# Layer-0 attention on one core: in each step of TensorE's loop the weighted sums are issued after the first score matmul, where they stood after the second

## The chip, the cores and the metric

The kernel runs on one core of one Trainium2 chip. The metric is the device time of one launch in microseconds. Lower is better. The kernel before has a median of 871.83 us over 3 runs.

## What is computed

The program is a two-layer block on an input of 2 x 1024 x 256. Layer 0 is a layer norm, an attention with 16 query heads of width 16 that share 8 key/value heads, and beside it a gated feed-forward whose weights are looked up in a table of 16 values. Layer 1 is a recurrence and a mixture of experts. Only the attention of layer 0 is touched:

```python
q = compute_rope(q); k = compute_rope(k)            # B, S, 16, heads
scores = einsum('bsdkg,btdk->bkgst', q, k) / sqrt(256)
w = softmax(scores, axis=-1)
ctx = einsum('bkgst,btdk->bkgsd', w, v)
```

and what reads it: the output projection, `x = x + s * silu(ffn)`, then layer 1, which needs that sum.

## The kernel before

Each engine runs a program of its own, written out by hand; semaphores tie the programs together. An engine takes its instructions in the order of the code, so the order on TensorE is the order of `attend_tensor`.

The attention is done in `NG` = 16 groups (2 batches x 8 key/value heads), each of `NTT` = 8 steps `t` of 128 keys. So there are 128 steps. One step of the main loop issues on TensorE:

- **maxima.** `maximum(k, h)` (line 879) computes 128 queries against 512 keys; two of them (`h` = 0, 1) fill two PSUM banks, and VectorE reduces the two banks to a maximum for each query (`row_max`, line 791). A step has two such pairs, `k` at its start and `k + 1` at its end. They run `NST + AHEAD` = 26 pairs ahead, for the next groups. There are two pairs of banks, so pair `k` waits until the reduction of pair `k - 2` is over.
- **scores.** `scores(n, t, i)` (line 891), `i` = 0 to 3, computes 128 keys against 512 queries, with the maximum subtracted by two more rows. ScalarE turns each into `probs_t` by an exponential (line 767). Three PSUM banks go round, so a score waits for the exponential of the score three before it (`pe.wait_ge(p_ready, k - 2)`).
- **weighted sums.** `weigh(n, t)` (line 903) multiplies the four `probs_t` of the step two steps back (`LAG` = 2) by the values, four matmuls that each go to their own 32 output partitions. The trace has two records for each of them, so eight.
- **early feed-forward.** `up_two` (line 924): in the last 12 steps, two matmuls of the next stage.

The operands of maxima and scores have 48 to 50 rows and lie twice, from partition 0 and from partition 64 (`HEAD_ROWS` = 64), one copy for each query head of the pair. I call the half from partition 0 half A, the other half B. `maximum(k, h)` takes half A for even `k` and half B for odd `k`. The scores 0, 1, 2, 3 of a step take halves B, B, A, A as long as there are maxima to compute; after that, in the last 13 steps, B, A, B, A (`paired`).

VectorE has besides the reductions one table lookup (`look_up`, line 822) in every second step of the groups 0 to 11, and in each group one transpose (line 800) and one reciprocal (line 635). The last 16 lookups and their additions run in the last two groups, after the last reduction. ScalarE has one copy of the sums out of PSUM for each group (`take_o`, line 629). The first thing that ScalarE does after its last exponential is `take_high` (line 738), on which the feed-forward stage waits.

Of the kernel before, what the change touches and what calls it, by code (L numbers as in the profile page):

```python
# [498 lines left out]
def attention_stage(nc, m, a):  # L499
# [59 lines left out]
    def paired(n, t):  # L559

        return (2, 3, 0, 1) if (n + 1) * NST + AHEAD + G * t < NG * NST else (2, 0, 3, 1)
# [3 lines left out]
    def pair(k):  # L565

        return 2 * (k % 4) if k < FIRST else 2 * (k % 2)

    def by_relu(k):

        return PLAIN <= k < FIRST
# [9 lines left out]
    def ring(i):  # L581
        return SP[i % 3]
# [267 lines left out]
    def attend_tensor(pe):  # L850
        m.project_tensor(pe)
        pe.wait_ge(m.ones_ready, NQK)

        def rows(g, n):
            return slice(g * HEAD_ROWS, g * HEAD_ROWS + n)

        def maximum(k, h):

            if k >= NG * NST:
                return  # L860
            n, i = divmod(k, NST)
            if i == 0 and h == 0:
                pe.wait_ge(qk_in[n % NQK], 16 * m.LOADS * (n // NQK + 1))
            back = 4 if k < FIRST else 2
            if k >= back and h == 0:
                pe.wait_ge(max_done, k - back + 1)
            if k == 1 and h == 0:

                pe.wait_ge(m.v_out, NT)
            if k == 2 and h == 0:  # L870

                pe.wait_ge(m.prod_q, 4 * NB)
                pe.wait_ge(m.prod_k, 2 * NB)
            st, g = divmod(i, G)
            keys = KS[n % NQK][rows(g, NROW), h * BLK:(h + 1) * BLK]
            if by_relu(k) and h == 0:
                pe.wait_ge(kd_in[n], 16 * G)
                keys = KD[n][rows(g, NROW), :]
            mm = nc.tensor.matmul(bank[pair(k) + h], QS[n % NQK][rows(g, NROW), st * P:(st + 1) * P], keys,  # L879
                                  start=True, stop=True)  # L880
            if h == 1:
                mm.then_inc(max_ps, 1)

        def scores(n, t, i):
            k = (n * NTT + t) * NJ + i
            g, half = divmod(paired(n, t)[i], NJ // G)
            if t == 0 and i == 0:
                pe.wait_ge(m_in, 16 * G * (n + 1))
            if k >= 3:
                pe.wait_ge(p_ready, k - 2)  # L890
            nc.tensor.matmul(ring(k)[:], KS[n % NQK][rows(g, NAUG), t * P:(t + 1) * P],  # L891
                             QS[n % NQK][rows(g, NAUG), half * BLK:(half + 1) * BLK],
                             start=True, stop=True).then_inc(s_ps, 1)

        def weigh(n, t):
            bb, kv = divmod(n, KV)
            for i in range(NJ):
                k = (n * NTT + t) * NJ + i
                j = paired(n, t)[i]
                pe.wait_ge(p_ready, k + 1)  # L900
                if t == 0 and i == 0 and n >= 1:
                    pe.wait_ge(o_done, n)
                nc.tensor.matmul(OB[32 * j:32 * (j + 1), :], m.VS[:, bb * NTT + t, kv, :], pt[:, k % NPT, :],  # L903
                                 start=(t == 0), stop=(t == NTT - 1)).then_inc(pv_done, 1)

        fh = m.fh[:, 0:KC * GUW].rearrange("p (c n) -> p c n", c=KC)
        fl = m.fl[:, 0:KC * GUW].rearrange("p (c n) -> p c n", c=KC)
        first = slice(0, BLK)

        def up_two(j):  # L910

            c, r = divmod(j, 6)
            w, r = divmod(r, 3)
            if j == 0:

                pe.wait_ge(f_hi, NPIECE)
                pe.wait_ge(f_lo, NPIECE)
                pe.wait_ge(max_done, NG * NST)
            cols = slice(w * FULL + c * P, w * FULL + (c + 1) * P)
            for i in (2 * r, 2 * r + 1):  # L920
                kc, term = divmod(i, 3)
                lhs = fl if term == 0 else fh
                rhs = m.xTl if term == 1 else m.xTh
                mm = nc.tensor.matmul(bank[2 * c + w][:], lhs[:, kc, cols], rhs[:, kc, first],
                                      start=(i == 0), stop=(i == 5))
            if j % 6 == 5:
                mm.then_inc(gu_ps, 1)

        for k in range(FIRST):
            maximum(k, 0)  # L930
            maximum(k, 1)
        for n in range(NG):
            for t in range(NTT):
                k = (n + 1) * NST + AHEAD + G * t
                for h in range(2):
                    maximum(k, h)
                scores(n, t, 0)
                scores(n, t, 1)
                if t >= LAG:
                    weigh(n, t - LAG)  # L940
                elif n >= 1:
                    weigh(n - 1, NTT - LAG + t)
                scores(n, t, 2)
                scores(n, t, 3)
                for h in range(2):
                    maximum(k + 1, h)
                early = n * NTT + t - (NG * NTT - 6 * NEARLY)
                if early >= 0:
                    up_two(early)
        for t in range(NTT - LAG, NTT):  # L950
            weigh(NG - 1, t)

    m.attend_sync, m.attend_gpsimd, m.attend_scalar, m.attend_vector, m.attend_tensor = (
        attend_sync, attend_gpsimd, attend_scalar, attend_vector, attend_tensor)
    m.take_o, m.pv_done, m.PV_ALL = take_o, pv_done, NG * NTT * NJ

# [2022 lines left out]
```

## Time and profile before

| | |
|---|---|
| time, median of 3 runs | 871.83 us (867.97 to 871.92) |
| profiled execution | 866.55 us, its span 864.7 us |
| mean granted TensorE clock | 0.945 |
| PE busy | 776.1 us (90%) |
| DVE (VectorE) busy | 701.9 us (81%) |
| ACT (ScalarE) busy | 537.8 us (62%) |
| POOL (GpSimd) busy | 330.4 us (38%) |

Busy shares are means over stages that differ. PE's matmul records have ends that are modelled, so a PE that is always busy is not a PE at its peak. In the timeline rows the first number is the start in us from the start of the span, the second the time taken by the instruction or by a run of equal ones, `xN` their number, and the bracket the idle time of the engine just before, with what ended it.

### The profile page before, as it was taken

The numbers are of one execution on the slowest core, as the hardware profiler recorded it, in microseconds if no ns is written. First come the engines' busy times: TensorE is split into PE (matmuls) and PEld (weight loads), VectorE is DVE, ScalarE is ACT, GpSimd is POOL, SyncE is SP. The second block draws the span as 40 slices with busy tenths as digits, with TensorE's granted clock in tenths as the row PEclk, the third lists the DMA queues.
The fourth block names the chain that finished last, engine by engine and source line by source line (L and its number), as shares of the span: only waits on it lengthen the run. The fifth ranks groups of instructions, "written<-read, shape, count | busy, mean of one in ns | idle before, by whom it ended". The sixth has DMA issues, their size and how long they took to land. (4 is left out here: it accounts for less than half of the span.)

```text
span 864.7 us, 18013 instructions
## 1 busy us (share of the span) xinstructions
PE 776.1 (90%) x6593; PEld 508.2 (59%) x6593; DVE 701.9 (81%) x1131; ACT 537.8 (62%) x988; POOL 330.4 (38%) x283
## 2 busy tenths in 40 slices
PE   3979999999999999999899998996668899999986
PEld 2865333333333333333388887986657587999875
DVE  4769999999999999999766676668999486666486
ACT  4527788887788888888844335445576353666442
POOL 5440444347544653021010000107787560444340
PEclk9985999999999999999999999998687699999999
DMA  6495532222222222000066000002006113444352
GB/s 240 172 217 165 191 89 52 52 52 53 51 53 52 52 52 52 16 16 17 20 202 127 2 1 13 2 1 70 5 11 270 69 63 60 123 124 134 114 161 74
DMA packets 60183, 71.16 MB, mean 82 GB/s; under 512 B 24864, under 2 KB 46496, under 8 KB 59712
## 3 DMA queue, kind: packets, MB, share of 16 engines
q1 hardware_dynamic: 56016, 59.31, 25.7%
q0 software_dynamic: 3408, 9.38, 3.1%
q10 hardware_dynamic: 672, 1.31, 0.5%
q8 instruction: 54, 0.88, 0.4%
q14 instruction: 33, 0.27, 0.1%
HBM read 40.47 MB, written 27.41 MB: 78 GB/s over the span
## 5 line engine op out<-in xcount | busy, mean ns | idle before, releaser
L767 ACT ACTIVATE probs_t<-psum 128x512 f32<-128x512 f32 x512 | 271.4, 601 | 65.5 <-PE psum L891 63.7
L791 DVE TENSOR_REDUCE row_max<-psum 128x1 f32<-128x1024 f32 x234 | 272.5, 1214 | 10.4 <-PE psum L879 9.9
L891 PE MATMUL psum<-QS,KS 50*128 50x512 f32 x512 | 194.5, 469 | 1.3 <-ACT probs_t L767 1.2
L879 PE MATMUL psum<-KS,QS 48*128 48x512 f32 x490 | 174.2, 457 | 13.6 <-DVE row_max L791 11.3
L701 POOL TENSOR_TENSOR lut_sum<-lut_sum,lut_tmp 128x1080 f32<-128x1080 f32 x45 | 112.3, 2496 | 131.0 <-DVE lut_tmp L822 131.0
L891 PEld LDWEIGHTS psum<-QS,KS 50*128 50x128 f32 x512 | 82.7, 188 | 135.2 <-ACT probs_t L767 127.8
L903 PE MATMUL psum<-probs_t,VS 128*32 128x512 f32 x1024 | 137.9, 611 | 1.1
L879 PEld LDWEIGHTS psum<-KS,QS 48*128 48x128 f32 x490 | 77.3, 195 | 54.0 <-DVE row_max L791 48.3
L2531 POOL DMA_INDIRECT y_rows<-y_slot,ids x39 | 37.5, 962 | 61.4 <-ACT y_slot L2594 61.1
L822 DVE TENSOR_SCALAR lut_tmp<-lut_idx,lut 128x1080 f32<-128x1080 int32 x60 | 47.5, 793 | 0.4
L1289 POOL TENSOR_TENSOR rstd<-var_eps,minus_half 128x4 f32<-128x4 f32 x8 | 8.4, 1045 | 99.9 <-DVE var_eps L1284 99.9
L903 PEld LDWEIGHTS psum<-probs_t,VS 128*32 128x32 f32 x1024 | 20.8, 108 | 36.5 <-ACT probs_t L767 19.6
L493 PE MATMUL psum<-xTh,ffn_l 128*128 128x512 f32 (+1 forms) x80 | 31.6, 395 | 2.4 <-DVE f_h L1149 2.4
L1388 POOL TENSOR_TENSOR key<-key,tot 128x512 f32<-128x512 f32 x24 | 29.9, 1260 | 8.7 <-PE psum L2295 6.0
L495 PE MATMUL psum<-xTh,ffn_h 128*128 128x512 f32 (+1 forms) x80 | 31.6, 395 | 0.0
L1094 ACT ACTIVATE f_silu<-psum 128x512 f32<-128x512 f32 (+1 forms) x24 | 14.3, 598 | 27.7 <-PE psum L495 27.7
L494 PE MATMUL psum<-xTl,ffn_h 128*128 128x512 f32 (+1 forms) x80 | 31.6, 395 | 0.0
L2690 DVE TENSOR_TENSOR xt_l<-psum,xt_h 128x256 fp32r<-128x256 f32 x39 | 16.6, 424 | 17.8 <-ACT xt_h L2601 17.6
L1101 ACT ACTIVATE f_hh<-f_h 128x512 fp32r<-128x512 f32 (+1 forms) x24 | 15.2, 632 | 24.3 <-DVE f_h L1149 21.0
L2594 ACT ACTIVATE y_slot<-psum,w_tile 128x256 f32<-128x256 f32 x39 | 18.6, 476 | 16.7 <-issue 10.3
L714 POOL TENSOR_SCALAR max_res<-row_max_t 128x32 f32<-128x32 f32 x16 | 5.8, 361 | 57.8 <-DVE row_max_t L800 57.6
L2295 PE MATMUL psum<-recept,key 128*32 128x64 f32 x1024 | 19.9, 238 | 8.8 <-issue 6.7
(333 smaller groups left out, 1902.1 us busy)
## 6 DMA issues: line engine op xcount, KB each, us to landing
KS<-k_rows SPq DMA_DIRECT2D x31, 192.0 KB, 4.5
QS<-q_rows SPq DMA_DIRECT2D x31, 192.0 KB, 5.0
x_rows<-zero_rows SPq DMA_DIRECT2D x1, 4992.0 KB, 17.7
x_slot<-x_rows SPq DMA_DIRECT2D x39, 128.0 KB
m_raw<-experts_w SPq DMA_DIRECT2D x2, 2432.0 KB
q_rows<-part SPq DMA_DIRECT2D x8, 512.0 KB, 5.2
y_token<-y_rows SPq DMA_DIRECT2D x8, 512.0 KB, 7.4
x_tok<-x SPq DMA_DIRECT2D x4, 512.0 KB, 8.8
```

The costliest lines, as they stand in the source:

```text
L493: nc.tensor.matmul(out, ll, rh, start=start and i == 0, stop=False)
L494: nc.tensor.matmul(out, lh, rl, start=False, stop=False)
L495: mm = nc.tensor.matmul(out, lh, rh, start=False, stop=stop and i == n - 1)
L701: nc.gpsimd.tensor_tensor(w, w, wtmp[:, slot % 2, :], ALU.add).then_inc(lut_add, 1)
L767: nc.scalar.activation(pt[:, k % NPT, :], ring(k)[:], ACT.Exp, scale=float(E) ** -0.5).then_inc(p_ready, 1)
L791: nc.vector.tensor_reduce(out, m.psum[:, j:j + 2, :], AX_XY, ALU.max).then_inc(max_done, 1)
L822: nc.vector.tensor_scalar(wsum[:, cols] if v == 0 else wtmp[:, slot % 2, :], idx[:, cols], float(v), lut[:, v:v + 1], ALU.is_equal, ALU.mu ...
L879: mm = nc.tensor.matmul(bank[pair(k) + h], QS[n % NQK][rows(g, NROW), st * P:(st + 1) * P], keys, start=True, stop=True)
L891: nc.tensor.matmul(ring(k)[:], KS[n % NQK][rows(g, NAUG), t * P:(t + 1) * P], QS[n % NQK][rows(g, NAUG), half * BLK:(half + 1) * BLK], sta ...
L903: nc.tensor.matmul(OB[32 * j:32 * (j + 1), :], m.VS[:, bb * NTT + t, kv, :], pt[:, k % NPT, :], start=(t == 0), stop=(t == NTT - 1)).then_ ...
L1388: nc.gpsimd.tensor_tensor(k[:, :, 0, :], k[:, :, 0, :], t[:, :, 1].unsqueeze(2).broadcast_to([P, S // (2 * s), s]), ALU.mult).then_inc(k_d ...
L2531: nc.gpsimd.indirect_dma_start(m.y_rows, bass.IndirectOffsetOnAxis(ap=ids[:, j:j + 1], axis=0), yo[:, j % 4, :], None).then_inc(ys_out[j % ...
```

## The change

The call of `scores(n, t, 1)` moves from ahead of the weighted sums to behind them. No instruction is added or removed, and only TensorE's order differs.

```diff
                 for h in range(2):
                     maximum(k, h)
                 scores(n, t, 0)
-                scores(n, t, 1)
                 if t >= LAG:
                     weigh(n, t - LAG)
                 elif n >= 1:
                     weigh(n - 1, NTT - LAG + t)
+                scores(n, t, 1)
                 scores(n, t, 2)
                 scores(n, t, 3)
                 for h in range(2):
```

The first place is TensorE in the middle of the attention, a step of the first groups. L891 are scores, L903 the weighted sums, L879 maxima (four in a row: the pair that ends a step and the pair that begins the next).

```order
 L879 MATMUL psum<-KS_78,QS_74 128x512 x4
-L891 MATMUL psum<-QS_72,KS_76 128x512 x2
-L903 MATMUL psum<-probs_t,VS 32x512 x4
-L891 MATMUL psum<-QS_72,KS_76 128x512 x2
+L891 MATMUL psum<-QS_72,KS_76 128x512
+L903 MATMUL psum<-probs_t,VS 32x512 x4
+L891 MATMUL psum<-QS_72,KS_76 128x512 x3
 L879 MATMUL psum<-KS_78,QS_74 128x512 x4
```

Between the weighted sums and the next maxima stand three scores, on halves B, A, A, where two stood, on A, A.

The second place is TensorE in the last group, where no maxima are left and two matmuls of the feed-forward (L924) stand at the end of each step.

```order
 L924 MATMUL psum<-xTh,ffn_l 128x512
 L924 MATMUL psum<-xTl,ffn_h 128x512
-L891 MATMUL psum<-QS_75,KS_79 128x512 x2
-L903 MATMUL psum<-probs_t,VS 32x512 x4
-L891 MATMUL psum<-QS_75,KS_79 128x512 x2
+L891 MATMUL psum<-QS_75,KS_79 128x512
+L903 MATMUL psum<-probs_t,VS 32x512 x4
+L891 MATMUL psum<-QS_75,KS_79 128x512 x3
 L924 MATMUL psum<-xTh,ffn_h 128x512
 L924 MATMUL psum<-xTh,ffn_l 128x512
```

Ahead of the weighted sums one score is left, on half B; behind them are three, on A, B, A, where two were, on B, A.

## Rows read from the trace of the kernel before

**Rows 1.** Costliest groups of the page: busy, mean ns, idle before.

```profile
L791 DVE TENSOR_REDUCE row_max<-psum 128x1 f32<-128x1024 f32 x234 | 272.5, 1214 | 10.4 <-PE psum L879 9.9
```

**Rows 2.** Busy time of each engine by stretch (us, instructions), granted clock.

```profile
100.00:200.00 100.00, 95.21 (x604) 33.96 (x603) 99.75 (x104) 82.86 (x159) 48.54 (x33) 1.00 0.29 63
200.00:340.00 140.00, 132.28 (x826) 47.36 (x824) 138.68 (x143) 112.22 (x214) 78.48 (x48) 0.99 0.24 50
340.00:390.00 50.00, 49.46 (x305) 17.85 (x302) 45.08 (x43) 41.47 (x80) 6.31 (x8) 1.00 0.14 30
392.00:424.00 32.00, 31.47 (x170) 10.93 (x167) 29.81 (x33) 26.68 (x50) 3.38 (x3) 1.00 0.06 12
428.00:520.00 92.00, 91.38 (x539) 78.90 (x540) 62.15 (x132) 37.45 (x58) 8.78 (x9) 1.00 0.32 79
```

**Rows 3.** Timeline of VectorE, two transposes and one stretch of reductions.

```profile
133.03 0.21 DVE L800 STREAM_TRANSPOSE row_max_t<-row_max 128x32 f32<-128x32 f32 x1
...
154.27 0.21 DVE L800 STREAM_TRANSPOSE row_max_t<-row_max 128x32 f32<-128x32 f32 x1
...
157.76 0.78 DVE L822 TENSOR_SCALAR lut_tmp<-lut_idx,lut 128x1080 f32<-128x1080 int32 x1
158.45 4.61 DVE L791 TENSOR_REDUCE row_max<-psum 128x1 f32<-128x1024 f32 x4
...
163.75 3.47 DVE L791 TENSOR_REDUCE row_max<-psum 128x1 f32<-128x1024 f32 x3
```

**Rows 4.** Timeline of PE over the same two steps.

```profile
159.90 0.50 PE L891 MATMUL psum<-QS,KS 50*128 50x512 f32 x1
159.90 0.49 PE L879 MATMUL psum<-KS,QS 48*128 48x512 f32 x1
160.23 0.39 PE L891 MATMUL psum<-QS,KS 50*128 50x512 f32 x1
160.24 0.39 PE L879 MATMUL psum<-KS,QS 48*128 48x512 f32 x1
160.85 0.49 PE L879 MATMUL psum<-KS,QS 48*128 48x512 f32 x1 [0.22 <-DVE row_max L791]
...
161.52 1.06 PE L903 MATMUL psum<-probs_t,VS 128*32 128x512 f32 x8
162.52 0.50 PE L891 MATMUL psum<-QS,KS 50*128 50x512 f32 x1
...
163.70 0.50 PE L891 MATMUL psum<-QS,KS 50*128 50x512 f32 x1
164.13 1.06 PE L903 MATMUL psum<-probs_t,VS 128*32 128x512 f32 x8
...
165.47 0.39 PE L879 MATMUL psum<-KS,QS 48*128 48x512 f32 x1
```

**Rows 5.** Timeline of ScalarE, the exponentials between those sums.

```profile
163.05 2.07 ACT L767 ACTIVATE probs_t<-psum 128x512 f32<-128x512 f32 x4 [0.31 <-PE psum L891]
```

**Rows 6.** Timeline of PE, one step of the last group.

```profile
412.67 0.50 PE L891 MATMUL psum<-QS,KS 50*128 50x512 f32 x2
413.10 0.50 PE L924 MATMUL psum<-xTh,ffn_h 128*128 128x512 f32 x1
413.44 0.39 PE L924 MATMUL psum<-xTh,ffn_l 128*128 128x512 f32 x1
413.76 0.60 PE L891 MATMUL psum<-QS,KS 50*128 50x512 f32 x2
414.29 1.06 PE L903 MATMUL psum<-probs_t,VS 128*32 128x512 f32 x8
```

**Rows 7.** Timeline at the end of the attention, ScalarE and PE.

```profile
423.64 1.09 ACT L767 ACTIVATE probs_t<-psum 128x512 f32<-128x512 f32 x2 [0.44 <-PE psum L891]
424.61 1.11 ACT L738 ACTIVATE ffn_h<-lut_sum 128x1080 fp32r<-128x1080 f32 x1
...
428.48 0.50 PE L493 MATMUL psum<-xTh,ffn_l 128*128 128x512 f32 x1 [2.35 <-DVE f_h L1149]
```

## The prediction

> **What bounds the kernel now.** I read the busy time by stretch first, to see which engine is full where. From 100 to 340 us VectorE is busy 99.75 of 100 us and 138.68 of 140 us; TensorE follows with 95% and ScalarE with 80 to 83% [rows 2]. That is the stretch of groups 0 to 11, in which VectorE has the table lookups beside its reductions. All its reductions together stood idle for only 10.4 us in the whole span [rows 1]. From 340 to 390 us the lookups are over, VectorE falls to 45.08 of 50 us, and TensorE is busy 49.46 us. From 392 to 424 us, without maxima, TensorE is busy 31.47 of 32 us [rows 2]. Behind the attention, TensorE is again busy 91.38 of 92 us [rows 2].
>
> The timelines say how. VectorE: a reduction takes 1.21 us [rows 1], and four in a row take 4.61 us, so they follow each other every (4.61 - 1.21) / 3 = 1.133 us. A lookup holds the next reduction up by 158.45 - 157.76 = 0.69 us. The lookup with the reciprocal holds it up by 163.75 - (158.45 + 4 x 1.133) = 0.77 us, so the reciprocal costs 0.08. From transpose to transpose it is 154.27 - 133.03 = 21.24 us [rows 3]: 16 reductions are 18.13, 4 lookups 2.76, and the 0.35 left are the reciprocal and a transpose of 0.27. The group's length is VectorE's own work and nothing else.
>
> TensorE: from weighted sums to weighted sums it is 164.13 - 161.52 = 2.61 us, and this is a ring. The first score behind the sums starts 1.00 later (162.52) [rows 4]; its exponential starts at 163.05 [rows 5]; it takes 0.60 (four take 2.07, two take 1.09 [rows 5, 7], so the spacing is 0.49 and one alone 0.60); its PSUM bank is then free, and the score three places on starts at 163.70, 0.05 behind its end; 0.43 later, at 164.13, the sums start [rows 4]. That is 1.00 + 0.53 + 0.60 + 0.05 + 0.43 = 2.61.
>
> **The change part by part.** It adds and removes nothing and moves one score per step past the sums, in all steps but the first two of group 0. Three stages answer differently.
>
> *The ring.* Before, the first score behind the sums is number 2, and the one three places on is number 1, the last ahead of the next sums. After, they are numbers 1 and 0, again the first behind and the last ahead. The ring has the same members and stays at 2.61 us. TensorE's bare work stays too: scores and maxima fill the two halves of the array side by side, and with score 1 moved behind, both halves still have four each. Cost 0 in the 19 steps from the end of the lookups to the last maximum (340 to 390 us), where VectorE has (50 - 45.08) / 19 = 0.26 us of air in a step.
>
> *The second pair of maxima in the VectorE-bound stretch.* Before, it starts in half B together with the first score in half A, at 159.90, though another score stands ahead of it in the program; its second matmul starts at 160.24 and ends at 160.63 [rows 4]. After, score 1 goes into half B first. What one more matmul in a half costs is in the same rows: the first score ends at 159.90 + 0.50 = 160.40, the second at 160.23 + 0.39 = 160.62, so 0.22 us. The pair is ready 0.22 later after the sums. Is there air for this? Two paths lead from a first reduction (start 158.45 + 1.133 = 159.58) to the second reduction two steps on.
> VectorE's own: five spacings and a lookup, 5.67 + 0.69 = 6.36 us, or 6.44 with the reciprocal and 6.63 with the transpose in it. TensorE's: the reduction ends at 160.79, the next maximum that waited for it starts at 160.85, the sums follow at 161.52 and, one ring later, at 164.13; the second pair starts its last matmul at 165.47, which ends at 165.86 [rows 4], and VectorE needs 0.03 more (163.02 to 163.05 between a score and its exponential [rows 4, 5]; I take the same). That is 6.31. The air is 0.05, 0.13 or 0.32 us, against 0.22 wanted: short by 0.17, 0.09, or not at all.
> These paths overlap, and a stall in one double step is air for the next. A group has four double steps: plain, transpose, plain, reciprocal. They stall by 0.17, 0, 0.17 and 0, so 0.34 us per group. The maxima of the next step wait for the reductions that have been moved, so the loss is kept: 12 groups x 0.34 = **+4.1 us**. Bounds: 0 if the air is really 0.2 us; 4 stalls of 0.17 in each group, 8.2 us, if a stall gives nothing back. One term I leave at nothing: score 3, which stands ahead of the second pair, waits for score 0's exponential, now the fourth behind the sums. It ends 0.53 + 3 x 0.49 + 0.60 = 2.60 us behind the sums, so that score 3 may start 2.65 - 2.61 = 0.04 behind the end of the next ones, where half A lets it stream from 0.33 on: in time by 0.29. Once a group the copy out of PSUM stands among these exponentials; at one more spacing (0.49) it makes score 3, and the pair behind it, 0.2 late, in an even step, whose second reduction has a lookup's 0.69 us ahead of it. If that cover is gone, it is 0.2 a group, +2.4.
>
> *The steps without maxima.* In each of the last 12, before: two scores side by side, feed-forward matmuls 0.43 and 0.77 later, scores at 1.09, sums at 1.62 (412.67, 413.10, 413.44, 413.76, 414.29 [rows 6]), next scores 1.00 after: 2.62 us. After: three scores stand behind the sums, on A, B, A; the third shares half A with the first and ends 0.22 later, which moves the feed-forward to 0.65 and the one score ahead of the sums to 0.65 + 0.34 + 0.32 = 1.31. Alone it needs 0.43 to the sums [rows 4], where the pair needed 0.53. Sum 1.31 + 0.43 + 1.00 = 2.74, so 0.12 more, x 12 = **+1.5 us**. Bounds: 0 if the third score hides; 0.33 a step, 4 us, if it costs a whole start-to-start distance (160.23 - 159.90). Behind the last sums three exponentials run where two did (1.09 us [rows 7]), one spacing more: **+0.5 us**. In the last group's copy step the third score is 0.2 late as above, with no lookup to cover it: **+0.2 us**. Together +2.2, bounds 0.5 to 4.7.
>
> *What passes on.* ScalarE goes from its last exponential straight into the copy of line 738 at 424.61, and TensorE stands 2.35 us until 428.48 for what comes of it [rows 7]. All of layer 1 needs x, and TensorE is full up to 520 us [rows 2]. So a late end of the exponentials passes on whole.
>
> Sum: 4.1 + 2.2 = **+6.3 us**. The profiled execution took 866.55 us and would take 872.9. It lies below all three timed runs (867.97 to 871.92), whose mean is 870.6; two of them are near 871.9. I forecast from that mean: 870.6 + 6.3 = **876.9 us**.
>
> *A rule, weighed.* A matmul of half B, later in the program, starts at 159.90, while a score ahead of it starts at 160.23 [rows 4]. The Trainium skill (TensorE: Matmul & The Clock Gate, Part 3 on packing small matmuls) states that matmuls start and end strictly in program order. By that rule the pair of maxima would already stand behind both scores before the change, and moving score 1 would cost the main stretch nothing, for a sum of +2.2 in place of +6.3; the starts in this trace disagree.
>
> **The rivals.**
> 1. *Likeliest, 0.60:* as above, +3.5 to +10 (876.9).
> 2. *VectorE's air is enough, 0.15.* A margin of 0.05 to 0.13 hangs on hundredths, and the reductions may be served late in a way that I can't see in starts alone. Then only the last steps cost: 870.6 + 2.2 = 872.8. Against it: the two paths come from start times that repeat in every double step.
> 3. *Halves in program order, 0.05.* If the later half-B matmul is shown at 159.90 but streams only with the score at 160.23, before and after are alike in the main stretch. Also 870.6 + 2.2 = 872.8. Against it stands the start at 159.90. (This is the case of the Trainium skill's rule above, TensorE: Matmul & The Clock Gate, Part 3.)
> 4. *Slower still, 0.12.* Score 3 waits for score 0's exponential in every step. By the spacings it is in time by 0.29. If the exponentials come 0.5 later than I reckon, the pair of maxima is 0.2 later in every step: the two stalls of each group grow by 0.2 each, 24 x 0.2 = 4.8, and 12 late feed-forward pairs add 2.4. That is +7.2 on case 1, about 884.
> 5. *Faster, 0.08.* Before, score 1 waits just ahead of the sums for an exponential. If score 0 does not, because ScalarE's first exponential behind the sums is done when TensorE asks for the bank, the ring opens. TensorE then needs only about 1.0 for maxima and scores, 0.1 and 1.00 for the sums, and the 19 steps from 340 us fall to VectorE's 2 x 1.133 = 2.27: 19 x 0.34 = -6.3, so 864.3. It decides itself at the start of the last score ahead of the sums: it would have to come under 1.0 us behind the end of the sums, where exponential and start give 0.53 + 0.60 + 0.05 = 1.18.
>
> **How the numbers follow.** About 0.5% (4.4 us) is what a measurement can tell from no change. Case 1 holds slower 0.54 and same 0.06; cases 2 and 3 same 0.17 and slower 0.03; case 4 slower 0.12; case 5 faster 0.07, same 0.01. Sums: faster 0.07, same 0.24, slower 0.69. The range 870.0 to 882.5 takes in case 1 with its bounds but the last of them, and cases 2 and 3; it leaves out 5 and most of 4. The likeliest case alone: 873.5 to 881.
>
> **What would show it.** In the profile after, transposes of groups 1 to 11 some 21.5 to 21.6 us apart (21.24 before). VectorE waiting for line 879 some 0.1 to 0.2 us about twice a group, below 99% busy. Steps from 340 to 390 us still 2.61. In the last 12 steps 2.74 from sums to sums. Three exponentials behind the last sums. The second pair of maxima ending 1.95 us after the sums start where it ended at 1.73. Wrong would be: that pair still at 1.73 (case 3), transposes still 21.24 apart (case 2), a ring other than 2.61 in the middle (4, 5), or a fall of the granted clock in another place than now, which would change one stretch by a few us and which I can't foresee.

## The result

| | before | after |
|---|---|---|
| median | 870.8 us (6 runs, 866.46 to 871.92) | 882.21 us (6 runs, 879.48 to 883.98) |
| ratio after / before | | 1.014, 95% interval 1.0116 to 1.0165 |
| profiled span | 864.7 us | 879.0 us |

The change makes the kernel 1.4% slower, 882.21 - 870.8 = 11.4 us where 6.3 were forecast. The direction was right, and the size was too small by almost half. The medians in this document are over all runs of a kernel, and one run in a slower state (887.58 us, of the kernel with the changed order in step 2 only) is left out of its ratio.

### The profile page after: what moved, and what is told of

Read it like the earlier page. It is cut to its first block and busy times, and to the rows that moved or that the text cites. A ratio compares the mean times of both kernels' runs of the same rounds, so it can differ in the third digit from the quotient of the medians.

```text
span 879.0 us, 18013 instructions
## 1 busy us (share of the span) xinstructions
PE 790.0 (90%) x6593; PEld 525.1 (60%) x6593; DVE 703.6 (80%) x1131; ACT 532.9 (61%) x988; POOL 330.6 (38%) x283
## 5 line engine op out<-in xcount | busy, mean ns | idle before, releaser
L767 ACT ACTIVATE probs_t<-psum 128x512 f32<-128x512 f32 x512 | 266.8, 604 | 83.2 <-PE psum L891 83.2
L891 PE MATMUL psum<-QS,KS 50*128 50x512 f32 x512 | 162.0, 480 | 2.4 <-ACT probs_t L767 2.4
L879 PE MATMUL psum<-KS,QS 48*128 48x512 f32 x490 | 154.2, 437 | 7.8 <-DVE row_max L791 3.5
L903 PE MATMUL psum<-probs_t,VS 128*32 128x512 f32 x1024 | 139.5, 618 | 6.2 <-ACT o_sb L629 6.2
L891 PEld LDWEIGHTS psum<-QS,KS 50*128 50x128 f32 x512 | 64.1, 188 | 132.4 <-ACT probs_t L767 125.3
L879 PEld LDWEIGHTS psum<-KS,QS 48*128 48x128 f32 x490 | 84.4, 198 | 45.3 <-DVE row_max L791 35.6
L903 PEld LDWEIGHTS psum<-probs_t,VS 128*32 128x32 f32 x1024 | 20.9, 108 | 43.9 <-ACT probs_t L767 36.1
```

The lines of the kernel that those rows point to most:

```text
L767: nc.scalar.activation(pt[:, k % NPT, :], ring(k)[:], ACT.Exp, scale=float(E) ** -0.5).then_inc(p_ready, 1)
```

## The profile after

The transposes on VectorE mark the groups, as in [rows 3]. First column start, second duration:

```profile
134.78 0.21 DVE L800 STREAM_TRANSPOSE row_max_t<-row_max 128x32 f32<-128x32 f32 x1
156.64 0.21 DVE L800 STREAM_TRANSPOSE row_max_t<-row_max 128x32 f32<-128x32 f32 x1
```

A group takes 156.64 - 134.78 = 21.86 us, where it took 21.24 and 21.58 was forecast. The sum of waits from 88 to 440 us (waiter, releaser: us in total, times, longest) has a row that the kernel before did not have (the second one; the first stood at 6.7 us, 16 times, there):

```profile
DVE row_max L791 <- PE psum L879: 13.6, 28, 1.5
PE psum L903 <- ACT o_sb L629: 6.2, 14, 0.6
```

The weighted sums wait for the copy of the group before out of PSUM (`take_o`, line 629), 14 times, 0.44 us each on average. One of these waits, TensorE's timeline after:

```profile
150.13 1.06 PE L903 MATMUL psum<-probs_t,VS 128*32 128x512 f32 x8
151.13 0.50 PE L891 MATMUL psum<-QS,KS 50*128 50x512 f32 x2
...
152.31 0.49 PE L891 MATMUL psum<-QS,KS 50*128 50x512 f32 x1
152.46 0.39 PE L879 MATMUL psum<-KS,QS 48*128 48x512 f32 x1
153.38 1.07 PE L903 MATMUL psum<-probs_t,VS 128*32 128x512 f32 x8 [0.52 <-ACT o_sb L629]
154.38 0.50 PE L891 MATMUL psum<-QS,KS 50*128 50x512 f32 x2
```

ScalarE over the same time:

```profile
151.66 1.08 ACT L767 ACTIVATE probs_t<-psum 128x512 f32<-128x512 f32 x2 [0.54 <-PE psum L891]
152.63 0.60 ACT L629 ACTIVATE o_sb<-psum 128x512 f32<-128x512 f32 x1
153.11 1.11 ACT L767 ACTIVATE probs_t<-psum 128x512 f32<-128x512 f32 x2
```

and VectorE:

```profile
154.40 0.77 DVE L822 TENSOR_SCALAR lut_tmp<-lut_idx,lut 128x1080 f32<-128x1080 int32 x1
155.38 1.23 DVE L791 TENSOR_REDUCE row_max<-psum 128x1 f32<-128x1024 f32 x1 [0.20 <-PE psum L879]
```

The sums that end around 151.13 complete a group. ScalarE sits idle for 0.54 us, does the exponentials of scores 1 and 2, then the copy, which ends at 153.23. The next sums start a new group in the same PSUM bank, so they wait for the copy and start at 153.38. They would have gone at about 152.31 + 0.43 = 152.74. The same place in the kernel before, TensorE and then ScalarE:

```profile
148.25 1.06 PE L903 MATMUL psum<-probs_t,VS 128*32 128x512 f32 x8
150.48 0.44 PE L891 MATMUL psum<-QS,KS 50*128 50x512 f32 x1
151.01 1.06 PE L903 MATMUL psum<-probs_t,VS 128*32 128x512 f32 x8
149.78 0.60 ACT L767 ACTIVATE probs_t<-psum 128x512 f32<-128x512 f32 x1 [0.53 <-PE psum L891]
150.27 0.59 ACT L629 ACTIVATE o_sb<-psum 128x512 f32<-128x512 f32 x1
```

There one exponential (score 2) stood between the sums and the copy, here there are two (scores 1 and 2). So the copy ended 150.86 - 148.25 = 2.61 us behind the start of the sums before, and ends 153.23 - 150.13 = 3.10 behind it now, one spacing of ScalarE (0.49) later. In both kernels the next sums start 0.15 behind the end of the copy: 2.76 and 3.25 us from sums to sums. Before, TensorE was busy with score 1 until 150.92, so that no idle time showed this wait.

After the change the second pair of maxima follows late (1.95 us behind the start of the sums, at 155.33), and VectorE stands 0.20 us despite the lookup ahead of it.

In the stretch without lookups, VectorE has less work to hide it behind. TensorE after, sums to sums:

```profile
392.88 1.07 PE L903 MATMUL psum<-probs_t,VS 128*32 128x512 f32 x8
395.49 1.07 PE L903 MATMUL psum<-probs_t,VS 128*32 128x512 f32 x8
398.74 1.07 PE L903 MATMUL psum<-probs_t,VS 128*32 128x512 f32 x8 [0.58 <-ACT o_sb L629]
401.35 1.06 PE L903 MATMUL psum<-probs_t,VS 128*32 128x512 f32 x8
```

The ring is 2.61 us as forecast, but one step in eight takes 3.25. In the kernel before that step took 2.76:

```profile
385.34 1.06 PE L903 MATMUL psum<-probs_t,VS 128*32 128x512 f32 x8
388.10 1.06 PE L903 MATMUL psum<-probs_t,VS 128*32 128x512 f32 x8
```

Last, a step of the last group after, to be held against [rows 6], on TensorE:

```profile
431.90 1.06 PE L903 MATMUL psum<-probs_t,VS 128*32 128x512 f32 x8
432.90 0.73 PE L891 MATMUL psum<-QS,KS 50*128 50x512 f32 x3
433.56 0.50 PE L924 MATMUL psum<-xTh,ffn_h 128*128 128x512 f32 x1
433.89 0.39 PE L924 MATMUL psum<-xTh,ffn_l 128*128 128x512 f32 x1
434.21 0.49 PE L891 MATMUL psum<-QS,KS 50*128 50x512 f32 x1
434.63 1.06 PE L903 MATMUL psum<-probs_t,VS 128*32 128x512 f32 x8
```

and the end of the exponentials on ScalarE:

```profile
436.16 1.57 ACT L767 ACTIVATE probs_t<-psum 128x512 f32<-128x512 f32 x3 [0.67 <-PE psum L891]
437.61 1.11 ACT L738 ACTIVATE ffn_h<-lut_sum 128x1080 fp32r<-128x1080 f32 x1
```

Sums to sums is 2.73 us (2.62 before), and the feed-forward starts 433.56 - 432.90 = 0.66 behind the first score (0.43 before). Three exponentials end the attention. Line 738 starts at 437.61, 13.0 us later than before [rows 7]. Where these come from, cut at the transposes: 0.5 us is there at the first transpose of the main loop (91.16 against 90.63), 8.3 come in the 11 group lengths up to the transpose at 336.62 (327.80 before), 2.0 in the three after it (65.38 against 63.36 us), 2.2 from the last transpose to line 738 (35.61 against 33.45). Of the 8.3, 11 x 0.62 = 6.8 are the steady excess. The rest, 1.5 us, lies around a stretch of the lower granted clock (0.50), which lasts from about 219.5 to 229.9 us in this execution and from 215.9 to 219.3 in that of before.

## The experiments

The theory after the result: two waits make the loss in the steps with maxima. One is forecast (the second pair of maxima is later), the other is not (the sums of step 2 wait for the copy). The rival is that one of them alone is the cause. The "group" below is the distance of two transposes in a stretch of full clock. Each kernel is compared with runs of the kernel before that were taken along with it; their medians were 869.88, 870.62 and 870.02 us.

**The copy earlier.** An edit on ScalarE on top of the change: the copy goes into the idle 0.54 us.

```diff
-                if i == LAG * NJ - 1 and n >= 1:
+                if i == NJ + 1 and n >= 1:
                     take_o(act, n - 1)
```

> The changed kernel, with one more edit on ScalarE: the copy of the sums out of PSUM stands before the exponential of score 1 of step 1 (the sums are over by then, and ScalarE idles 0.54 us there), where it stood before that of score 3. Theory A, the wait for this copy (6.2 us idle ahead of the sums, 14 times) is the part of the loss that the prediction did not have: groups 21.55 us from transpose to transpose (21.86 now, 21.24 before), no wait of the sums for the copy, the three groups without lookups 2.0 us shorter, in all 6 us off, near 876. Rival, the late second pair of maxima would have stalled VectorE by then anyway: groups stay at 21.8, only the groups without lookups and the last one gain, 2 to 2.5 us off, near 880.

Measured: 875.45 us, ratio to before 1.0067 (1.0043 to 1.0091). The transposes:

```profile
134.29 0.21 DVE L800 STREAM_TRANSPOSE row_max_t<-row_max 128x32 f32<-128x32 f32 x1
155.84 0.21 DVE L800 STREAM_TRANSPOSE row_max_t<-row_max 128x32 f32<-128x32 f32 x1
```

The group is 21.55 us, the forecast number, and the wait for the copy is gone from the sum of waits. The three groups up to the last transpose, most of them without lookups, take 64.11 us (65.38, and 63.36 before); they are 1.27 shorter where 2.0 was expected. The copy's wait is 0.31 us of each group's 0.62.

**The copy later.** The opposite dose.

```diff
-                if i == LAG * NJ - 1 and n >= 1:
+                if i == LAG * NJ and n >= 1:
                     take_o(act, n - 1)
```

> The changed kernel with the copy out of PSUM one exponential later than it is (before that of score 0 of step 2), the suspected wait made longer by one exponential, 0.49 us. Theory A: the sums of step 2 wait about 1.0 us where they wait 0.5, 14 times; groups without lookups 0.49 longer (22.4), groups with lookups 0.3 to 0.49 longer (22.2 to 22.35), 5 to 7 us over the changed kernel, near 888. Rival (the sums' wait is not what makes the groups long): no difference, 882.

Measured: 896.94 us, ratio 1.0305 (1.0251 to 1.0359), 9 us more than the 888 expected. TensorE at the waiting sums:

```profile
155.30 0.49 PE L891 MATMUL psum<-QS,KS 50*128 50x512 f32 x1
155.40 0.39 PE L879 MATMUL psum<-KS,QS 48*128 48x512 f32 x1
156.85 1.93 PE L903 MATMUL psum<-probs_t,VS 128*32 128x512 f32 x8 [1.06 <-ACT o_sb L629]
```

Busy time around it (stretch, length, then PE, its weight loads, VectorE, ScalarE, GpSimd; the granted clock is the column before the last two):

```profile
150.00:156.80 6.80, 5.79 (x35) 2.31 (x35) 6.69 (x7) 5.47 (x12) 2.60 (x2) 1.00 0.60 116
156.80:160.20 3.40, 3.35 (x16) 1.39 (x16) 1.36 (x2) 1.05 (x3) 1.96 (x1) 0.51 0.14 31
160.20:170.00 9.80, 9.37 (x62) 3.58 (x59) 9.46 (x10) 7.71 (x15) 3.79 (x5) 1.00 0.06 10
```

The wait is 1.06 us here, 13.2 us over 14 times, as expected. Where the clock stays up a group takes 22.35, also as expected (22.2 to 22.35). But behind four of the 14 waits the granted clock falls from its upper level (2.4 GHz) to 0.51, the lower one (1.2 GHz): three times for 3.4 us, as here, where the eight records of the sums take 1.93 us in place of 1.06 and the group 23.9, and once, from 300.2 us, for 6.9. The five groups concerned (23.91, 23.89, 23.90, 23.63 and 23.74) are together 7.3 us above 22.35 each, which is most of the 9 us. The other ten waits, five of them of 1.01 to 1.07 us, were not followed by a fall, so the length of the wait alone does not decide it, and what does is not shown.

**The pair of maxima first in its half.** On top of the change, the scores take halves B, A, A, B in place of B, B, A, A, and the second pair is issued between them; the copy stays where it was.

```diff
-        return (2, 3, 0, 1) if ...
+        return (2, 0, 1, 3) if ...
...
                 scores(n, t, 1)
+                maximum(k + 1, 0)
                 scores(n, t, 2)
+                maximum(k + 1, 1)
                 scores(n, t, 3)
-                for h in range(2):
-                    maximum(k + 1, h)
```

> The changed kernel, but in the steps with maxima the scores take halves B, A, A, B instead of B, B, A, A, and the second pair of maxima is issued between them (score 1, maximum, score 2, maximum, score 3), so that after the sums it is first in half B again. Theory B, the later pair costs 0.3 us a group: the pair ends 1.73 us behind the start of the sums (1.95 now), groups 21.55 (21.86 now, the copy's wait stays), 3.5 us off, near 878.5. Rival, the copy's wait is all of the loss: groups stay at 21.86, 882.

Measured: 877.55 us, ratio 1.0075 (1.0049 to 1.0102). The transposes:

```profile
138.44 0.21 DVE L800 STREAM_TRANSPOSE row_max_t<-row_max 128x32 f32<-128x32 f32 x1
160.01 0.21 DVE L800 STREAM_TRANSPOSE row_max_t<-row_max 128x32 f32<-128x32 f32 x1
```

and TensorE behind one step's sums (which start at 153.70):

```profile
154.69 0.50 PE L891 MATMUL psum<-QS,KS 50*128 50x512 f32 x1
154.70 0.50 PE L879 MATMUL psum<-KS,QS 48*128 48x512 f32 x1
155.03 0.39 PE L891 MATMUL psum<-QS,KS 50*128 50x512 f32 x1
155.03 0.39 PE L879 MATMUL psum<-KS,QS 48*128 48x512 f32 x1
```

The pair ends 155.03 + 0.39 - 153.70 = 1.72 us behind the start of the sums, and the group is 21.57 us. The late pair is 0.29 us of a group; with the copy's 0.31 that makes 0.60 of the 0.62 found. The 65.38 us up to the last transpose become 64.90.

**Both, and the last 13 steps as before.** The two edits above, the order of before from the point where no maxima are left, and the copy before the exponential of score 2 in the last group.

```diff
+                one = k < NG * NST
                 scores(n, t, 0)
+                if not one:
+                    scores(n, t, 1)
...
+                if one:
+                    scores(n, t, 1)
+                    maximum(k + 1, 0)
                 scores(n, t, 2)
+                if one:
+                    maximum(k + 1, 1)
                 scores(n, t, 3)
```

> Both edits together, the early copy and the pair of maxima first in half B, and the last 13 steps in the order of before (there the copy stands before the exponential of score 2). One score, weighted sums, three scores is left in the 115 steps with maxima. If the three causes are all there is, it equals the kernel before: groups 21.24, steps without lookups 2.61, near 871. Rival, the order itself costs something that I have not named: groups over 21.4, 874 or more.

Measured: 870.6 us, ratio 1.0001 (0.9967 to 1.0035). Its transposes:

```profile
132.05 0.21 DVE L800 STREAM_TRANSPOSE row_max_t<-row_max 128x32 f32<-128x32 f32 x1
153.21 0.21 DVE L800 STREAM_TRANSPOSE row_max_t<-row_max 128x32 f32<-128x32 f32 x1
```

One score, sums, three scores in the 115 steps with maxima costs nothing that can be told, once its followers are put right. The group is even 21.16 us, 0.08 less than before: the kernel before had one small stall per group, four reductions in 4.68 us where this kernel has 4.61 throughout. The row of the kernel before:

```profile
147.73 4.68 DVE L791 TENSOR_REDUCE row_max<-psum 128x1 f32<-128x1024 f32 x4
```

In the whole time 11 x 0.08 = 0.9 us can't be told from no change. The three groups up to the last transpose take 63.33 us, as before (63.36).

**The last 13 steps alone, from both sides.** First the changed order only while there are maxima, then only in the last 13 steps.

```diff
+                one = k < NG * NST        # the other kernel: k >= NG * NST
                 scores(n, t, 0)
+                if not one:
+                    scores(n, t, 1)
...
+                if one:
+                    scores(n, t, 1)
                 scores(n, t, 2)
```

> The changed order only in the 115 steps that still have maxima; the last 13 steps have the order of before. By the traces the last stretch cost 2.2 us, so 2 us off the changed kernel, near 880, transposes 21.86 apart and the last steps 2.61. Rival, that stretch is covered by VectorE's last lookups and additions: no difference, 882.

> The order of before, with the changed order only in the last 13 steps. The same term from the other side: 2.74 from sums to sums in the last steps, three exponentials behind the last sums, 2.2 us over the kernel before, near 873. Rival (covered): 871.

Measured: 878.78 us, ratio 1.0107 (1.0073 to 1.0141), and 872.28 us, ratio 1.0018 (0.9995 to 1.0042). From the last transpose to line 738 the first takes 33.75 us and the second 35.09 (33.45 before, 35.61 after the change). The sums of the second kernel in that stretch:

```profile
418.90 1.07 PE L903 MATMUL psum<-probs_t,VS 128*32 128x512 f32 x8
421.64 1.07 PE L903 MATMUL psum<-probs_t,VS 128*32 128x512 f32 x8
```

2.74 us each, as forecast. The stretch costs 35.09 - 33.45 = 1.6, 35.61 - 33.75 = 1.9 or 35.61 - 33.45 = 2.2 us in the traces. It is not cleanly cut out: where the order changes, five scores stand between two sums in the first kernel (3.08 us from sums to sums, at 401.20) and three in the second (1.90, at 391.11). By its device time the second kernel can't be told from the one before, so this term rests on the traces.

**Step 2 alone, from both sides.** The changed order in all steps but step 2, and in step 2 only, meant to single out the sums that wait for the copy.

```diff
+                one = t != LAG            # the other kernel: t == LAG
                 scores(n, t, 0)
+                if not one:
+                    scores(n, t, 1)
...
+                if one:
+                    scores(n, t, 1)
                 scores(n, t, 2)
```

> The changed order in all steps but step 2 of each group, which has the order of before (two scores, sums, two scores). In step 2 the sums wait for the copy out of PSUM. Theory A: as the kernel with the early copy, near 876, groups 21.5 to 21.6, because one more score ahead of the sums covers the copy. Rival (the pair of maxima is all): one step of eight less of the new order, 1/8 of the loss off, near 881.

> The order of before, with the changed order only in step 2 of each group. Theory A: the wait for the copy is there (0.5 us, 14 or 15 times), and costs 0.1 to 0.3 us a group in the 12 groups that VectorE bounds and 0.4 to 0.6 in the four others: 2.5 to 5 us over the kernel before, near 874.5. Rival (the pair of maxima is all): 1/8 of the loss, 872.

Measured: 879.62 us, ratio 1.0102 (1.007 to 1.0135), and 882.35 us, ratio 1.0101 (1.0046 to 1.0156). Both expectations failed. The second kernel has the changed order in one step of eight, and is as slow as the changed kernel in the median; its runs scatter from 873.91 to 887.58. The groups are 21.65 and 21.66 us. The sums of the first kernel, on TensorE:

```profile
148.52 1.06 PE L903 MATMUL psum<-probs_t,VS 128*32 128x512 f32 x8
...
151.76 1.07 PE L903 MATMUL psum<-probs_t,VS 128*32 128x512 f32 x8
...
153.88 1.06 PE L903 MATMUL psum<-probs_t,VS 128*32 128x512 f32 x8
```

Here five scores stand between two sums, and it is 3.24 us from one to the next, not 2.61. The last of the five waits for the exponential of the second behind the sums, which is one spacing later in ScalarE's row, and the sums then start 0.14 behind the end of the copy. Three scores stand ahead of the next sums, which follow after 2.12 us, so most of it comes back on TensorE (5.36 for two steps, against 5.22). In the second kernel the copy wait comes first (2.75 us from sums to sums at 355.06, with 0.44 idle) and the five scores after it (3.10). So neither kernel takes the copy wait out, or puts it in, alone, and they don't separate the causes. The ratio of the first is below the changed kernel's, but the intervals overlap.

**The copy earlier in the kernel before.** `i == NJ + 2` in place of `i == LAG * NJ - 1`, nothing else.

> The kernel before with the copy out of PSUM before the exponential of score 2 of step 1 in place of score 3's. In the old order the copy made the sums of step 2 late by 0.15 us; VectorE hides that in 12 groups, so at most 0.5 us off in the last four: same, 870.5.

Measured: 869.89 us, ratio 0.9985 (0.9959 to 1.0011), no difference that can be told, as expected.

## Why the prediction was right or wrong

**Right: the bounds and the ring.** VectorE sets the pace up to 340 us (still 98.26 of 100 us busy from 100 to 200) and the ring of 2.61 us behind it. Both are in the profile after, and the ring did not change with the order.

**Right: the second pair of maxima.** It ends 1.95 us behind the start of the sums, as forecast, and without this lateness the group is 0.29 us shorter (0.34 forecast, 4.1 us in all; 11 x 0.29 = 3.2 by the experiment). The case of matmuls in program order is out: with it, the kernel with the early copy would have the group of before, 21.24 us, and it has 21.55. Case 4 is out too, though its 884 us lies nearer to the 882.21 measured than the likeliest case's 876.9: it wanted the pair 0.2 later still in every step, and the pair ends at 1.95.

**Right: the last steps, with some luck in their sum.** 2.73 to 2.75 us a step (2.74 forecast) and three exponentials at the end. From the last transpose on it is 2.2 us in all (2.2 forecast). But the copy step in it takes 3.25 us where it took 2.75 before, 0.5 and not 0.2 more, and the first sums behind the last transpose come 0.2 us sooner after it than before, which makes up for most of that.

**Wrong: the step in "One term I leave at nothing".** It named the copy out of PSUM among the exponentials, but asked only what score 3 loses by it. It did not ask what else waits for the copy. `weigh(n, t)` has a wait of its own at the first step of a group, `pe.wait_ge(o_done, n)`. With score 1 behind the sums, its exponential stands between the sums and the copy too, and the copy ends 3.10 us behind their start in place of 2.61. The kernel before had the same wait, 0.15 us past the ring and covered by score 1, so that no row showed it as idle; now the sums stand idle for 0.44 us on average, 14 times. In the 12 groups with lookups this costs 0.31 us each (11 x 0.31 = 3.4 us). In the groups without them it shows almost whole, 3.25 against 2.76 us in one step of eight. The forecast "cost 0 in the 19 steps" fails with it: the three groups that hold them are 2.0 us longer, of which the early copy takes off 1.27. The 64.11 - 63.36 = 0.75 that stays is the late pair's, since it is gone (63.33) when the pair is first in its half as well. So the air that the prediction saw in these steps does not cover the pair either. The first of the three groups, which still has two lookups, loses 0.34 of it, the other two 0.25 and 0.16; through which reductions was not traced.

**The claim that a group is VectorE's own work and nothing else** was off by 0.08 us, which was a stall too. Two products of the prediction are rounded the wrong way, 12 x 0.12 = 1.4 (not 1.5) and 19 x 0.34 = 6.5 (not 6.3); nothing hangs on them. That the stated range (870.0 to 882.5) still holds 882.21 is luck: its upper part came from bounds on other terms than the one that failed.

**The sum.** 6.8 + 2.0 + 2.2 = 11.0 us from the traces, against 11.4 measured. With the copy early the same count gives 11 x 0.31 + 0.75 + 1.7 = 5.9, against 875.45 - 869.88 = 5.6 measured; with the pair first in its half 11 x 0.33 + 1.5 + 2.4 = 7.5, against 6.9.

What stays open is how much of the difference between single executions comes from falls of the granted clock. Eight of the eleven profiles have one between 214 and 243 us, which lasts 3.4 us in the kernel before and 10.4 in the changed one, and three have none there. It comes some 5 to 6 us behind the start of a lookup that takes 2.4 us, beside GpSimd's longer work, where others take 0.8; but all eleven profiles have this long lookup. No run here shows what makes the fall long, short or absent.

## What to carry to other kernels

When an instruction is moved away from in front of another, list every wait that the second one has, not only the one that shows. A wait can be hidden by the instruction that leaves, and then no row of the profile has it. Ask also what is in the other engine's queue ahead of the release, and whether the move adds to it: here it put one more exponential ahead of the copy, and the cure was to put ScalarE's copy into an idle half microsecond that it already had. Where two engines hand banks to and fro in a fixed rotation, keep the number of hand-overs between two fixed points equal from step to step; five scores where there were four made that distance one more spacing, 0.49 us, longer at once (3.10 against 2.61).

## What the runs showed of the hardware

- Matmuls on the two halves of the array don't start in program order. In [rows 4] a maximum of half B starts at 159.90, ahead of the score of half A at 160.23 that precedes it in the program; and when one more score went into half B ahead of it, it was 0.22 us later (it ends 1.95 us behind the start of the sums, 1.73 before), which it would not have been if it had stood behind both scores anyway. The Trainium skill (TensorE: Matmul & The Clock Gate, Part 3) has matmuls start strictly in order; the starts in this case disagree.
- One more matmul of 512 columns in a half costs 0.22 us at full clock: two scores in half A end at 160.40 and 160.62 in [rows 4], and the pair of maxima in half B moved from 1.73 to 1.95 us.
- Some waits of about 1 us on TensorE, in a stream that is busy otherwise, were followed by the lower granted clock, most were not. In the kernel with the late copy, of eight waits of 1.01 to 1.07 us three were followed by 3.4 us at 0.51, with the sums at 1.93 us in place of 1.06, and five by none. Of its six shorter waits one (0.74 us) was followed by 6.9 us at 0.50. None of the 14 waits of 0.16 to 0.58 us in the changed kernel was followed directly by a fall. So a wait that grows by 0.5 us cost a group 2.0 us (23.9 against 21.86) where the clock fell for 3.4 us and 0.49 where it did not.
